# A deformable-convolution kernel: statistics as pivoted sums on ScalarE, a fifth product buffer, and group means one slot later

## What is computed

```python
def _gn(v, G=32, eps=1e-5):
    g = v.reshape(B_, H_, W_, G, C_ // G)
    m = jnp.mean(g, axis=(1, 2, 4), keepdims=True)
    s = jnp.var(g, axis=(1, 2, 4), keepdims=True)
    return ((g - m) / jnp.sqrt(s + eps)).reshape(v.shape)

x = x + deformable_conv(_gn(x), dw_w, dw_b, om_w, om_b, vp_w, vp_b, op_w)   # layer 0
x = x + binary_conv(_gn(x), kernel, bias)                                    # layer 1
```

## Time and profile before

| | |
|---|---|
| runs | 3857.94 us median (3854.49 to 3858.15) |
| profiled execution | 3859.76 us, span 3858.0 us |
| TensorE busy | 3628.5 us, 94% |
| VectorE busy | 3510.0 us, 91% |
| ScalarE busy | 2286.0 us, 59% |
| GpSimd busy | 565.0 us, 15% |
| multiplications L1026 | 800, 1811.2 us |
| transposing sums L796 | 12800, 1527.2 us |

### The profile page before, as it was taken

The page is one execution under the profiler, slowest core; times in us unless marked ns, Lnnn a source line. Parts: engine busy times, 40 slices in busy tenths (PEclk is TensorE's granted clock), DMA queues, the critical chain, the costliest instruction groups (busy, mean ns, idle before and its releaser), DMA issues. The chain is left out here.

```text
span 3858.0 us, 90635 instructions
## 1 busy us (share of the span) xinstructions
PE 3628.5 (94%) x37696; PEld 2369.5 (61%) x37696; DVE 3510.0 (91%) x2757; ACT 2286.0 (59%) x4547; POOL 565.0 (15%) x412
## 2 busy tenths in 40 slices
PE   4899999999999999999999999999999999858998
PEld 2566666666666666666666666666666666623333
DVE  4899999999999999999999999989999999948776
ACT  5556665666666665666556666665566666235554
POOL 0011111101111111111111001111111111104444
PEclk9999999999999999999999999999999999979999
DMA  6454565445555555455545555555544554345563
GB/s 177 100 111 102 110 125 132 101 111 116 124 120 109 114 123 115 94 108 127 131 99 119 112 121 114 107 122 131 118 100 97 106 107 94 52 158 199 209 215 147
DMA packets 319939, 470.35 MB, mean 122 GB/s; under 512 B 37244, under 2 KB 242684, under 8 KB 313736
## 3 DMA queue, kind: packets, MB, share of 16 engines
q0 software_dynamic: 94080, 196.11, 28.4%
q1 hardware_dynamic: 224584, 266.07, 23.2%
q10 hardware_dynamic: 832, 2.10, 0.1%
HBM read 262.53 MB, written 67.41 MB: 86 GB/s over the span
## 5 line engine op out<-in xcount | busy, mean ns | idle before, releaser
L1026 DVE TENSOR_TENSOR pv<-val,wsum 128x2048 f32<-128x2048 f32 x800 | 1811.2, 2286 | 21.4 <-ACT xdw L557 14.6
L796 PEld LDWEIGHTS ps_add<-ident,pv 128*128 128x128 f32 x12800 | 1401.2, 142 | 356.0 <-issue 223.7
L796 PE MATMUL ps_add<-ident,pv 128*128 128x128 f32 x12800 | 1527.2, 275 | 70.9 <-DVE pv L1026 62.7
L751 PE MATMUL ps_om<-xdw,omw 128*32 128x256 f32 x13824 | 868.4, 384 | 30.4 <-ACT hat L587 29.4
L585 ACT ACTIVATE hat<-ps_om,omb 128x256 f32<-128x256 f32 x576 | 276.0, 479 | 551.2 <-PE ps_om L751 501.9
L979 DVE TENSOR_TENSOR prod<-hat,mwy 128x1536 f32<-128x1536 f32 (+1 forms) x384 | 526.0, 1397 | 82.9 <-DMA wsum<-prod 61.8
L472 POOL DMA_DIRECT2D wsum<-prod x192 | 226.0, 1254 | 2556.8 <-DVE wsum L979 2556.8
L751 PEld LDWEIGHTS ps_om<-xdw,omw 128*32 128x32 f32 x13824 | 391.2, 109 | 330.2 <-issue 95.5
L589 ACT ACTIVATE msk<-ps_om,omb 128x256 f32<-128x256 f32 x288 | 137.0, 476 | 401.4 <-PE ps_om L751 399.3
L965 DVE TENSOR_TENSOR mwy<-hat,msk 128x768 f32<-128x768 f32 x288 | 274.4, 953 | 94.3 <-ACT hat L599 94.3
L722 PE MATMUL ps_bg<-tri,diag 128*32 128x512 f32 x3024 | 346.5, 592 | 11.9 <-ACT tri L551 11.9
(11 more groups left out here) (134 smaller groups left out, 2622.7 us busy)
## 6 DMA issues: line engine op xcount, KB each, us to landing
wsum<-prod POOLq DMA_DIRECT2D x160, 768.0 KB, 7.1
tri<-in_x_dram SPq DMA_DIRECT2D x725, 128.0 KB, 2.9
win<-in_x_dram SPq DMA_DIRECT2D x144, 256.0 KB, 3.6
x<-xres SPq DMA_DIRECT2D x128, 256.0 KB, 5.1
xres<-in_x_dram POOLq DMA_DIRECT2D x124, 256.0 KB, 8.4
out_dram<-c_x SPq DMA_DIRECT2D x31, 1024.0 KB, 4.5
c_x<-x SPq DMA_DIRECT2D x30, 1024.0 KB, 5.3
c_box<-box_d SPq DMA_DIRECT2D x16, 1024.0 KB, 7.4
```

Source lines behind the costliest of these rows:

```text
L751: mm = nc.tensor.matmul(ps_om[G * q:G * q + G, (par + i) % 2, 0:TOK], omw[:, h, comp, :], xdw[:, j % 2, h, q, :], start=h == 0, stop=h == ...
L796: mm = nc.tensor.matmul(ps_add[:, tb, c, :], pv[:, (j + uv) % PBUF, c, P * tb:P * tb + P], consts["ident"][:, :], start=uv == 0 and c % 4 ...
L1026: nc.vector.tensor_tensor(pv[:, (j + uv) % PBUF, :, :].rearrange("p c (r w) -> p c r w", w=W), val[:, :, SR * j + u:SR * j + u + SR, v:v + ...
```

## The change

It has four parts.

First, both statistics go from VectorE's bn_stats to ScalarE: a pass of `Identity` with a bias of minus a pivot (the first element of the channel) and an accumulator output gives the sum about the pivot, a pass of `Square` the sum of squares. VectorE makes mean and variance from the sums. The step statistics stand at the end of ScalarE's slots 1 and 2 (one half of the channels each), the sums ahead at the end of slots 7 and 0. The store of `xres` waits for the statistics as before.

Second, buffers: `PBUF` is 5. `acc` is no longer a tensor of its own but lies in `xres`, so that `summed` (slot 4) must wait until the store of the step before has read it; the wait in `keep_x2` goes.

Third, the loads ahead both go to `acc_t`. Half 0 is issued by GpSimd behind tap 6, ahead of tap 7, once the last projection has read `acc_t`; half 1 behind the residual, once ScalarE has summed half 0.

Fourth, the group means and the first part of the scales are made a slot later, and `aggregate` moves from slot 1 to slot 3 of step 1.

```diff
-PBUF = 4
+PBUF = 5
-    return dw(0) + only(means, "mean", (0, 0)) + dw(1) + dw(2) + only(means, "mean", (1, 1)) + ...
+    return dw(0) + dw(1) + only(means, "mean", (0, 0)) + dw(2) + only(means, "mean", (1, 1)) + ...
...
-        acc = sb("acc", [P, TB, Q, GC, G])
         acc_t = sb("acc_t", [P, CH, Q * TOK])
-        ahead = [acc[:, :, :, :, :].rearrange("p b q c g -> p (b q c g)"),
-                 acc_t[:, :, :].rearrange("p h t -> p (h t)")]
+        ahead = acc_t[:, :, :].rearrange("p h t -> p (h t)")
         xres = sb("xres", [P, CH, Q, TOK])
+        acc = xres[:, :, :, :].rearrange("p h q t -> p (h q t)")\
+            .rearrange("p (b q c g) -> p b q c g", b=TB, q=Q, c=GC)
...
-        MEANS_AT = [1, 3]
-        SCALES_AT = [0, 2, 4, 6]
+        MEANS_AT = [2, 3]
+        SCALES_AT = [1, 2, 4, 6]
...
# GpSimd
-                    nc.gpsimd.dma_start(ahead[half], ...).then_inc(x_ahead[half], 16)
+                    if half == 1:
+                        pool.wait_ge(sums_made, CH * CH * n + CH * j + 1)
+                    nc.gpsimd.dma_start(ahead, ...).then_inc(x_ahead[half], 16)
...
                         for k in SENT_TAPS:
+                            add_products(n, j, k)
                             if k == 6 and j < CH and n < NI - 1:
-                                load_ahead(n, j, 0, "back3")
-                            add_products(n, j, k)
+                                load_ahead(n, j, 0, "project3")
+                        if (n, j) != (0, 0):
+                            add_residual(*previous(n, j), unit(n, j, "project3", NI) + 1)
                         if j < CH and n < NI - 1:
                             load_ahead(n, j, 1, "project3")
-                        if (n, j) != (0, 0):
-                            add_residual(*previous(n, j), unit(n, j, "project3", NI) + 1)
...
# ScalarE
                 def summed(s):
                     act.wait_ge(add_done, SHIFTS * (s + 1))
+                    at_least(act, x2_stored, 16 * Q * s)
...
                 def keep_x2(s, u, at, par):
-                    if u == 0:
-                        at_least(act, x2_stored, 16 * Q * s)
...
+                def statistics(n, j, halves):
+                    ...
+                    for oh in halves:
+                        for i, kind in ((0, ACT.Identity), (1, ACT.Square)):
+                            nc.scalar.activation(spare[:, :, :], xres[:, oh, :, :], kind, bias=pivot2[:, oh:oh + 1],
+                                                 accum_out=x2_sums[:, oh, i, j:j + 1]).then_inc(stats2, 1)
+                            act.wait_ge(stats2, 2 * CH * s + 2 * oh + i + 1)
+                def sums_ahead(n, j, half):
+                    act.wait_ge(x_ahead[half], 16 * (CH * n + j + 1))
+                    ...
+                    nc.scalar.activation(ahead, ahead, ACT.Identity, bias=pivot[:, j:j + 1],
+                                         accum_out=x_sums[:, half, j, 0:1]).then_inc(centred, 1)
+                    act.wait_ge(centred, i + 2 + half)
+                    nc.scalar.activation(ahead, ahead, ACT.Square, accum_out=x_sums[:, half, j, 1:2]).then_inc(sums_made, 1)
...
+                        if k == AHEAD_AT and j < CH and has_next(n):
+                            sums_ahead(n, j, 0)
+                        if k == 0 and j in (1, 2) and has_next(n):
+                            sums_ahead(n, j - 1, 1)
+                        if k in (1, 2) and not is_step(n, j, 0, 0) and not is_step(n, j, 0, 1):
+                            statistics(*previous(*previous(n, j)), (k - 1,))
...
# TensorE and VectorE
-                 ... pv[:, (j + uv) % PBUF, ...]
+                 ... pv[:, (SHIFTS * j + uv) % PBUF, ...]
...
# VectorE, scales_ahead part 0
-                        for h in range(CH):
-                            nc.vector.bn_aggr(mv1[:, h, :], bs1[:, h, :, :]).then_inc(gx_step, 1)
-                        after(3, nc.vector.tensor_copy(mean1[:, :], mv1[:, :, 0]))
+                        after(1, ... tensor_tensor(mv1, x_sums[:, 0, :, :], x_sums[:, 1, :, :], ALU.add))
+                        after(2, ... tensor_scalar(mv1, mv1, 1.0 / HW, None, ALU.mult))
+                        after(3, ... tensor_tensor(var1, mv1[:, :, 0], mv1[:, :, 0], ALU.mult))
+                        after(4, ... tensor_tensor(mv1[:, :, 1], mv1[:, :, 1], var1, ALU.subtract))
+                        after(5, ... tensor_tensor(mean1, mv1[:, :, 0], pivot, ALU.subtract))
```

More of the change, by code:

```diff
@@ L95, in dw @@
         return only(first, "first", shares(FIRST_VALUES, u, DW_UNITS)) + only(not last, "dw", (u,))
-    return dw(0) + only(means, "mean", (0, 0)) + dw(1) + dw(2) + only(means, "mean", (1, 1)) + dw(3) + values(0) + only(not first, "back", range(4)) + values(1) \
+    return dw(0) + dw(1) + only(means, "mean", (0, 0)) + dw(2) + only(means, "mean", (1, 1)) + dw(3) + values(0) + only(not first, "back", range(4)) + values(1) \
         + only(not first, "project", range(4)) + values(2) + values(3)
@@ L210, in layer0 @@
         msk = sb("msk", [P, 2, TOK])
-        over = sb("over", [P, 2, TOK], BF16)
+        spare = sb("spare", [P, Q, TOK], BF16)
+        over = spare[:, 0:2, :]
         over_sum = sb("over_sum", [P, 2, TAPS])
@@ L227, in layer0 @@
         gx_tri = sb("gx_tri", [KROWS, CB, 2, CH])
-        bs1 = sb("bs1", [P, CH, HW // 512, 6])
+        pivot = sb("pivot", [P, CH])
+        x_sums = sb("x_sums", [P, 2, CH, 2])
         mv1 = sb("mv1", [P, CH, 2])
@@ L454, in load_ahead @@
                         pool.wait_ge(bg_full, unit(n, j, "dw3", NI) + 1)
-                    nc.gpsimd.dma_start(ahead[half], src[:, HW // 2 * half:HW // 2 * (half + 1)]).then_inc(x_ahead[half], 16)
+                    if half == 1:
+                        pool.wait_ge(sums_made, CH * CH * n + CH * j + 1)
+                    nc.gpsimd.dma_start(ahead, src[:, HW // 2 * half:HW // 2 * (half + 1)]).then_inc(x_ahead[half], 16)
                 def add_residual(n, j, units):
@@ L595, in hats @@
                         at_least(act, over_done, STEPS * n + j - 1)
-                    nc.scalar.activation(over[:, :, :], hat[:, par, :, 1, :], ACT.Relu, bias=consts["minus1"][:, 0:1],
+                    nc.scalar.activation(over, hat[:, par, :, 1, :], ACT.Relu, bias=consts["minus1"][:, 0:1],
                                          accum_out=over_sum[:, j % 2, k:k + 1]).then_inc(w0_done, 1)
@@ L624, in keep_x2 @@
                                          ps_bg[:, par, :], ACT.Copy).then_inc(bg_free, 1)
+                def statistics(n, j, halves):
+                    s = STEPS * n + j
+                    if is_step(n, j, NI - 1, STEPS - 1):
+                        act.wait_ge(bg_free, unit(n, j, "project3", NI) + 1 + BACK_UNITS + (PJ_UNITS if 1 in halves else PJ_UNITS // 2))
+                    else:
+                        act.wait_ge(xres_added, 16 * Q * (s + 1))
+                    if j == 0 and 0 in halves:
+                        at_least(act, mv_kept, n)
+                        nc.scalar.activation(pivot2[:, :], xres[:, :, 0, 0], ACT.Copy, scale=-1.0).then_inc(pivots_kept, 1)
+                        act.wait_ge(pivots_kept, n + 1)
+                    for oh in halves:
[3 more added lines that the diff above has]
+                            act.wait_ge(stats2, 2 * CH * s + 2 * oh + i + 1)
                 def keep_mean(n, j, i):
@@ L630, in keep_mean @@
                         .then_inc(bg_free, 2)
+                def sums_ahead(n, j, half):
+                    act.wait_ge(x_ahead[half], 16 * (CH * n + j + 1))
+                    i = 3 * (CH * n + j)
+                    if half == 0:
+                        nc.scalar.activation(pivot[:, j:j + 1], ahead[:, 0:1], ACT.Copy, scale=-1.0).then_inc(centred, 1)
+                        act.wait_ge(centred, i + 1)
+                    nc.scalar.activation(ahead, ahead, ACT.Identity, bias=pivot[:, j:j + 1],
+                                         accum_out=x_sums[:, half, j, 0:1]).then_inc(centred, 1)
+                    act.wait_ge(centred, i + 2 + half)
+                    nc.scalar.activation(ahead, ahead, ACT.Square, accum_out=x_sums[:, half, j, 1:2]).then_inc(sums_made, 1)
                 act.wait_ge(first_step, 5)
@@ L702, in _ @@
                 steps_of_images(act, step)
+                statistics(NI - 1, STEPS - 2, (0, 1))
                 summed(STEPS * NI - 1)
@@ L706, in _ @@
                     keep_back(u, at + u, u % 2)
+                statistics(NI - 1, STEPS - 1, (0,))
+                statistics(NI - 1, STEPS - 1, (1,))
             @block.tensor
@@ L919, in _ @@
                 dve.wait_ge(diag_made, CH * CB * 3 + 1)
-                def sums_ahead(n, j, half):
-                    dve.wait_ge(x_ahead[half], 16 * (CH * n + j + 1))
-                    for i in range(HW // 1024):
-                        last = nc.vector.bn_stats(bs1[:, j, HW // 1024 * half + i, :], ahead[half][:, 512 * i:512 * i + 512])
-                    last.then_inc(sums_made, 1)
```

(2 more changed lines are left out.)

71 lines of the change are left out of this document (34 added, 37 removed).

## The result

The changed kernel takes 3875.06 us (median of 7 runs, 3871.75 to 3878.40), the kernel before, beside it on the same chip, 3858.15 us. The ratio is 1.0043 [1.0031, 1.0055]: slower by 17 us. The forecast was 3886 us. The span of the profiled execution is 3873.2 us, 15.2 more than before.

A forecast was written before the change was run, and what follows sets the result against it. TensorE and VectorE both taken as full. Stalls of 13.45 us per image against 9.7 now: 26 over seven images, 2 at the end, on 3859.8 less 1.8: 3886 us. Narrow range 3867 to 3912 (0.44); eight in ten, 3822 to 3932.

The forecast's parts named there:

- The loads ahead of tap 7: GpSimd's queue, steps 0 and 1 of seven images: tap 7 lands late and stalls TensorE 4.3 us a step, bounds 1.9 to 5.2.
- How it reaches TensorE: Sign, steps 0 and 1: VectorE's tap 8 products wait some 8 us for the DMA, then TensorE for pv.
- The relief of VectorE: Statistics taken off VectorE: some 21 us per image, of which only 7.4 us reaches TensorE; ceiling 68 us over seven images.
- Rival (a): Tap 7 costs TensorE nothing and VectorE's relief arrives: 3826 us, chance 0.24.
- Added to ScalarE: Statistics passes in slots 1 and 2: 2.5 us per half, 0.1 stall a slot; sums ahead in 7 and 0: 4.3, zero.
- Rival (d): ScalarE is the new bound, halves taking 3.5 instead of 2.5 us, or Square needing another table: +62, 3948 us, chance 0.06.
- The rule against it: Adds and multiplies belong on VectorE: by it alone moving the sums ahead loses about 1.8 us in each half.
- The store that `summed` waits for: ScalarE's slot 4 waits for the x2 store: median hidden, worst 2.0 us; 0.1 per step, 0.4 per image.
- rival (c): The forecast holds and the store is late as well, 1.5 us in 31 steps more: 3930 us, chance 0.13.
- The fifth buffer: VectorE's wait for a free product buffer: between 0 and 5 us over the kernel, taken as zero.
- the group means a slot later: TensorE's same two matmuls and waits: zero beyond 0.25 and 0.8 us already counted in the step with the means.
- The clock: TensorE's granted clock may drop after new waits of 2 to 3 us: taken as zero, 14 places at 1 us in range.

The follow-up runs named there:

- experiment 4: The changed kernel in its own order (load of half 0 ahead of tap 7), but that load brings only 1/16 of the half: 3843.28 us.
- experiment 1: The changed kernel with one edit: GpSimd issues tap 7 ahead of the load of half 0: 3818.65 us, ratio 0.9896.
- experiment 8: The kernel before without its bn_stats in the loop, nothing added to ScalarE: 3804.77 us, ratio 0.9858.
- Experiment 9: experiment 1 with a third ScalarE pass over 128x1024 in each half of the step statistics: 3897.92 us, ratio 1.0101.
- experiment 6: experiment 1 with four product buffers for five: 3818.59 us, ratio 0.9895.
- experiment 7: experiment 6 with the old bn_stats put back on VectorE, on data already there, results unread; ScalarE keeps its passes: 3858.01 us, ratio 0.9996.
- Experiment 2: experiment 1, but GpSimd waits for the last projection before issuing tap 7; the load of half 0 stays behind it: 3835.62 us, ratio 0.9939.
- experiment 3: Experiment 2 with a load of half 0 that brings only 1/16 of it: 3836.55 us, ratio 0.9942.

## Why the prediction came out as it did

The direction and the mechanism were right, and the time is 11 us under the forecast, inside its narrow range.

**The loads ahead of tap 7.** This step carried the forecast: 4.3 us in each of 14 steps, 60 us. It measures 4.3 us in each of 13 places, 56 us; in the very first step the load waits for something else. Its parts were right too. The issue was forecast 9.4 us into slot 6 and is at 9.34. The hold behind 1 MB was forecast as 2.4 us and is 2.3 between experiment 4 and the changed kernel. The wait was to cost 1.9; with a small load ahead it is 2.0. The rows that it used put the start of the products at 16.27 + 2.1 + 2.4 = 20.8 us into slot 6 (16.27 is 1601.46 - 1585.19), for 20.78 measured, and the last start that costs nothing at 16.27 + 0.2 = 16.5, for the 16.5 of the table under experiment 4.

One reading in it does not generalise. The tap 7 issued 7.26 us into its slot is the latest of the kernel before between 600 and 3000 us; at the 11 places with a load its median is 5.77, and with the statistics gone from VectorE it is 3.28. So tap 7's issue is late by 6.1 us against experiment 1 and not by 2.1, and VectorE's spare there is about 4.5 us and not 0.2. The sum is not hurt by this, for the prediction took lateness and spare from the same row, and a lead of VectorE adds about the same to both.

**How it reaches TensorE.** VectorE was to wait "some 8 us" for the DMA, and waits 8.54 and 8.23; TensorE was to wait for `pv` in slots 8 and 0, and does so by 1.97, 0.95 and 0.96 us.

**The relief of VectorE.** The prediction counted 7.4 of the 9.7 us per image as VectorE's, 52 us in seven images, and experiment 8 gives 54.9. The whole 9.7, 68 us, was no reachable ceiling: without any statistics on VectorE 10.2 us of waits for hats in 2400 stay, as in the kernel before. Rival (a), the change without the cost of the order, was put at 3826 us; experiment 1 is that case, at 3818.65, and below the lower end of the range, 3822, which the prediction called the middle of (a).

**Added to ScalarE.** The sizes were good. The grouped instructions of the changed kernel, 600 to 3000 us:

```profile
L647 ACT ACTIVATE spare<-xres,pivot 128x1024 bf16<-128x1024 f32 x92 | 105.3, 1145 | 1.8
...
L664 ACT ACTIVATE acc_t<-acc_t,pivot 128x2048 f32<-128x2048 f32 x22 | 44.3, 2013 | 0.4
L667 ACT ACTIVATE acc_t<-acc_t 128x2048 f32<-128x2048 f32 x22 | 42.2, 1917 | 0.7
```

A half of the sums ahead lasts from 1403.39 to 1407.75, 4.3 us as forecast; `Square` without a bias costs 1.917 where `Identity` with one costs 2.013. The Trainium skill, page "ScalarE: Activation LUTs", section "What ACT_TABLE_LOAD costs", gave an estimate of 1.99 for the longer pass and 1.13 for the shorter, and the trace agrees to 0.03. The place was judged right too: the passes were said to be "at the edge" at 0.1 us a slot. Experiment 9 shows that edge, since one more pass costs its whole length. The 14 us between experiments 1 and 8 are 2.0 per image, and the prediction's terms for them (0.2 in the first interval, 0.8 + 0.25 in the second, 0.1, 0.2: 1.55 per image) come near: the four intervals differ by 0.13, 1.22, 0.49 and 0.15.

Rival (d) had `Square` asking for another activation table. The whole kernel has one load of a table, as before, now at line 670:

```profile
L670 ACT ACT_TABLE_LOAD x1 | 1.3, 1283 | 0.8 <-PEq L1918 0.8
```

**The rule against it.** By the Trainium skill, page "ScalarE: Activation LUTs", section "Rules for kernel authors", adds belong on VectorE rather than ScalarE. The trace agrees on the price of a pass and not on the verdict: 4.3 us on ScalarE for 2.5 on VectorE, and the kernel gains 40 us by it (experiments 6 and 7), because VectorE's time was on the path and most of ScalarE's was not.

**The 11 us between forecast and result.** The second interval was to be 6.95 over 99.47 and is 5.64 in the image shown, 5.75 over the six. The rows of the changed kernel:

```profile
1513.85 2.90 PE L840 MATMUL ps_add<-ident,pv 128*128 128x128 f32 x16 [2.06 <-DVE pv L1064]
...
1526.18 1.96 PE L840 MATMUL ps_add<-ident,pv 128*128 128x128 f32 x16 [0.52 <-DVE pv L1064]
...
1562.38 1.07 PE L795 MATMUL ps_om<-xdw,omw 128*32 128x256 f32 x16 [0.84 <-ACT hat L596]
```

Products cost 2.06 + 0.52 and a sum slowed from 1.97 to 2.90, 3.5 us for the 4.3 forecast. The 0.8 for the hats is there, as 0.84. The 0.5 left for the next DMA chain is not. Over the six images the order costs 4.07 us in this interval, and what experiment 1 has over its first interval, 1.7, stands for the 2.15 forecast for hats, means and a loss in ScalarE. The mean image is 417.28 us for 418.55 forecast, 9 us in seven images. Start and end of the kernel were forecast to lose 2 us and have gained 2.7. Together this is 13 to 14 us, where forecast and trace are 13 apart (28 for the 15.2 of the span).

**The store that `summed` waits for.** Forecast at 0.1 us a step with 1.5 as the rival (c). It costs nothing that the trace shows. The first sum of slot 4 waits 0.34 for 0.26 in the first two steps of an image, but ScalarE's copy ahead of it (first row below) is held by TensorE's last sum and not by a store, there and in every other step of the layer. The stores of line 388, 1400 to 1800 us, against the earlier trace rows:

```profile
1464.58 1.94 ACT L616 ACTIVATE xres<-ps_add 128x1024 f32<-128x1024 f32 x2 [0.73 <-PE ps_add L840]
...
DMA to landing us min/median/max: 2.3/3.0/4.8
```

They land in 3.0 us at the median for 5.8, and the prediction, which took the 5.8, had them done only 10.2 us into slot 3. Its argument, "no tri loads stand before it any more", is not what the program does: SyncE's order is the same in both kernels, and the store stands behind two tri loads in both. What differs is the time between them. SyncE in the kernel before (two rows) and in the changed kernel (two rows), the last issue ahead of the store and the store:

```profile
1537.47 0.60 SPq L373 DMA_DIRECT2D tri<-in_zeros_dram  x1
1538.35 2.35 SPq L381 DMA_DIRECT2D x<-xres  x4
...
1546.11 0.60 SPq L380 DMA_DIRECT2D tri<-in_zeros_dram  x1
1560.74 2.64 SPq L388 DMA_DIRECT2D x<-xres  x4
```

Before, the store was issued right behind the loads; now it waits for ScalarE's second half and is issued 14 us after them. The Trainium skill, page "DMA: Bandwidth & Descriptors", section "Queues, rings and completion order", says that descriptors of SyncE's queue are consumed in ring order on each DMA engine. The trace fits it here, though no run parts the loads from the other transfers of that time.

**The fifth buffer** and **the group means a slot later**: zero forecast. The buffer measured 0.06 us (experiment 6). The means were not tried by themselves, but the wait tables of 600 to 3000 us tell something. TensorE waits 3.0 us at the group means in the kernel before, and not at all in experiment 8 (means at the old place, VectorE relieved) nor in experiment 7 (means later, VectorE loaded). Either alone removes the wait, so moving them is worth nothing beside the relief, and saves up to 4 us without it.

**The clock.** Taken at zero, because the first sum after the 2.69 us wait of the earlier trace rows ran at 1.97 us. That row was one of six, and the 1.00 of the earlier trace rows is rounded: two slow sums of the kernel before (1011.22 and 1943.77) lie in its stretch. The kernel before waits exactly 2.69 us for `pv` at six places between 600 and 3000 us, and these are three of them:

```profile
700.50 2.95 PE L796 MATMUL ps_add<-ident,pv 128*128 128x128 f32 x16 [2.69 <-DVE pv L1026]
...
1115.92 1.97 PE L796 MATMUL ps_add<-ident,pv 128*128 128x128 f32 x16 [2.69 <-DVE pv L1026]
...
1943.77 3.60 PE L796 MATMUL ps_add<-ident,pv 128*128 128x128 f32 x16 [2.69 <-DVE pv L1026]
```

Three of the six sums ran at full clock and three did not. In the changed kernel the slow sums take 6.0 us more in 2400, where experiment 1 has none: 7 of the 56 us of the order are spent in them. They seem not to come on top of the waits. The changed kernel's row under experiment 4 gives the same 16.5 as the row above it, which has no slow sum, and at 1513.85 two waits and the slow sum come to 3.5 us, where at 1410.07 three waits come to 3.9: a slow sum takes the place of waiting for the next products. Against the kernel before, with its 4.6, they nearly cancel, and the mean granted clock is 0.986 for 0.987.

## What to carry to other kernels

When a load is put ahead of other DMAs in one queue, count three things for what stands behind it: how long the queue's engine waits for the load's own buffer, how long the load's data holds what follows, and when the engine that waits for it must begin so that nothing is lost. Take lateness and spare from the same row: a lead that the change adds enlarges both and drops out, and mixed rows do not agree. A relief of a full engine is worth what its partner can take up; here it gave 40 us, and one line's place in a queue took back 56. When an experiment moves a wait from one name to another, ask what else was late at the same moment before giving the cost to the name: take that cause away alone, and see whether the time goes or only the name.

## What was not expected of the hardware

- Two waits that overlap are shown as one. Experiment 2 has 30.6 us for hats and 1.7 for products, and experiment 3 17.2 and 14.3, at the same time of 3836 us and with products that begin equally late (17.84 and 18.02 us into slot 6).
- A DMA that stands first in the queue holds the next by its data, not by being there. Tap 8's products begin 9.11 us after tap 7's issue behind 64 KB (median of 11), about as without a load ahead (8.99 and 9.22 in experiments 2 and 3), and 11.44 behind 1 MB.
- TensorE's clock after a wait does not follow from the length of that wait. After the same 2.69 us, the sums of sixteen matmuls took 1.97 us or 2.84 to 3.60. The mean granted clock from 1513.8 to 1516.8 us, over one of these sums in the changed kernel, is 0.65 of full speed, so part of the stretch ran at 1.2 GHz and part at 2.4. What separates the cases stays open.
